# Adding the output bias by an adding transfer instead of by matmuls, in an adaLN block with a gated recurrence and experts

## The chip, the cores and the metric

One core of a Trainium2 chip runs the whole kernel. The metric is device time in microseconds (us) of one execution. Its engines have short names in the profile: PE is TensorE (PEld its weight loads), DVE is VectorE, ACT is ScalarE, POOL is GpSimd, SP is SyncE, which here only issues transfers.

## What is computed

The input x has 4 samples of 2048 tokens with 256 channels. The part that the change touches is the first half, the gated linear recurrence and its residual:

```python
h = _layernorm(x, axis=-1) * (1 + ca) + sa
x = x + ga * _L0_attn_ref(h, ...)          # ends with: return h @ W_out + b_out
h = _layernorm(x, axis=-1) * (1 + cb) + sb
x = x + gb * _L0_ffn_ref(h, ...)           # 8 experts, each takes 512 tokens of a sample
```

Inside the recurrence stand three products (input, gate a, gate x), a scan along the tokens, and the output product with its bias. `ga` is a vector for each sample (kept at least 0.25 from zero), so `ga * (h @ W_out + b_out)` is `h @ (W_out * ga) + ga * b_out`. The second half chooses tokens by a softmax over 8 experts, and runs two-layer experts on them.

## The kernel before

The kernel has two blocks, one after the other. The first (the recurrence stage, up to about 358 us) works on 16 groups of 512 tokens (NG = 16, 4 groups to a sample, GB = 4), each group as 4 tiles of 128 tokens (TT = 4). The second block is the expert layers and runs to the end.

The first block is a software pipeline. In step s (the loop variable `s`) the engines work on five groups at once: group a = s is loaded and normalised, c = s - 1 goes through the three products, r = s - 2 through the scan, d = s - 3 through the output product and the residual, e = s - 4 through the expert scores. Each engine has its own program, written out by hand; semaphores order them, and each engine takes its instructions strictly in turn.

TensorE, in step s: the transposes of the normalised rows of c (into psT), the transposes of x1 of e, `project(d)` (line 1205), the product with Wa (which waits for `lo_z` of c), the product with Wx, the scores of e, and the product with Wu. From step 9 on, the choice of the first sample's tokens goes along: a search bit by bit, for which VectorE compares (line 217), TensorE sums the hits by a tiny matmul (line 293), and VectorE decides (lines 224 to 229), four rounds in a step. The first count of a step is issued in the middle of the product with Wa.

VectorE, in step s: `gated_u(r)` (lines 863 and 870; it waits for ScalarE's root `sc_t` and for the product with Wu), `lo_z(c)` (852), `scan(r)` (883), `residual(d)` (894, it adds the output product in psO to the rows of x in `x_buf`, and takes statistics), `stats1(a)`, `clip(c)` (901), `norm1(a)` (842, it waits for GpSimd's `rstd1(a)`), in step 1 `setup_out` (line 1007 on), and `keep_scores(e)` (908). The rows of x stay as they were loaded, in one of five buffers `x_buf`, until the residual; `norm1` writes its result to `z1`. SP loads a buffer again when the residual of five groups before is done.

ScalarE, in step s: `hi_z(c)`, then `gate_a(c)` (tanh and two exps of the product with Wa), `gate_x(c)` and the root for the scale (791), with table loads between them. GpSimd has little to do: `rstd2(d)` (lines 684 to 690) on the statistics of the residual, then `rstd1(a)` (675 and 677). At the end, in step NG + 2, it issues the first gathers of expert rows (line 440), in `fetch`.

The bias `ga * b_out` reaches the output on TensorE: `setup_out` makes `bias_hi` and `bias_rows`, where rows 0 to 63 hold the rounded part and rows 64 to 127 the rest of the bias of each sample, and `pick`, a 128 x 128 matrix with ones in rows 0 and 64. In `project` a matmul of `pick` with `bias_rows` opens the accumulation of each tile (line 1213), before two products of h with Wout (line 1215; each is recorded as two). psO is one accumulator, so `project(d)` waits for residual(d - 1).

Of the kernel before, what the change touches and what calls it, by code (L numbers as in the profile page):

```python
# [6 lines left out]
F32 = mybir.dt.float32  # L7
F32R = mybir.dt.float32r
BF16 = mybir.dt.bfloat16
I32 = mybir.dt.int32  # L10
ALU = mybir.AluOpType
# [3 lines left out]
P = 128  # L15
# [33 lines left out]
def adaln_kernel(nc, x, W_in, b_in, W_gx, b_gx, W_ga, b_ga, a_param, W_out, b_out, gate_w, w1, w2, c, wmod, out):  # L49
    B, S, D = x.shape  # L50
# [30 lines left out]
    with keep:  # L81
# [3 lines left out]
        def sem(name):  # L85
            return keep.enter_context(nc.semaphore(name))
# [367 lines left out]
        def sbr(name, shape, dt=F32):  # L454
            return recur.enter_context(nc.sbuf_tensor(name, shape, dt))
# [28 lines left out]
        Wx = [sbr(f"Wx{q}", [P, KD, D], F32R) for q in range(2)]  # L484
        Wa = [sbr(f"Wa{q}", [P, KD, D], F32R) for q in range(2)]
        Wout = [sbr(f"Wout{n}", [P, KD, D]) for n in range(2)]
        bias_hi = sbr("bias_hi", [P, B, D], F32R)
        bias_rows = sbr("bias_rows", [P, B, D], F32R)
        pick = sbr("pick", [P, P], F32R)
        Gb = sbr("Gb", [P, B, KD, E])  # L490
        sb_bc = sbr("sb_bc", [P, B, E])
        ca1 = sbr("ca1", [P, B, KD])
# [85 lines left out]
        r_p = sem("scaled_u_ready")  # L578
        r_b = sem("b_ready")
        r_hs = sem("h_ready")  # L580
        r_O = sem("out_in_psum")
        r_x1 = sem("x1_ready")
        r_st2 = sem("stats2_read")
# [21 lines left out]
        with nc.Block() as block:  # L605
# [53 lines left out]
            def _(pool):  # L659
# [10 lines left out]
                def rstd1(g):  # L670
# [5 lines left out]
                    pool.wait_ge(r_rs1, 2 * g + 1)  # L676
                    pool.tensor_tensor(rs1[g % 2][:], ve1[:], mhalf[:], ALU.pow).then_inc(r_rs1, 1)

                def rstd2(g):

                    pool.wait_ge(r_mv2, g + 1)
                    if g >= 1:
                        pool.wait_ge(r_nm2, 2 * g)
                    pool.tensor_scalar(ve2[:], x1[g % 2][:, :, D + 1], EPS, None, ALU.add).then_inc(r_rs2, 1)  # L684
                    pool.wait_ge(r_rs2, 2 * g + 1)
                    pool.tensor_tensor(x1[g % 2][:, :, D + 1], ve2[:], mhalf[:], ALU.pow).then_inc(r_rs2, 1)
                    pool.wait_ge(r_rs2, 2 * g + 2)
                    pool.tensor_tensor(ve2[:], x1[g % 2][:, :, D], x1[g % 2][:, :, D + 1], ALU.mult).then_inc(r_nm2, 1)
                    pool.wait_ge(r_nm2, 2 * g + 1)
                    pool.tensor_scalar(x1[g % 2][:, :, D], ve2[:], -1.0, None, ALU.mult).then_inc(r_nm2, 1)  # L690

                pool.wait_ge(s_one, 5)
                for s in range(LAST + 1):
# [13 lines left out]
                        rstd2(d)  # L707
                    if a is not None:
                        rstd1(a)
                    if s == NG + 2:  # L710
                        fetch(pool, 0)
                fetch(pool, 1)
# [95 lines left out]
            def _(dve):  # L808
# [78 lines left out]
                def residual(g):  # L887

                    dve.wait_ge(r_O, g + 1)
                    if g >= 2:  # L890
                        dve.wait_ge(r_x1s[g % 2], 16 * (g // 2))
                        dve.wait_ge(r_T2, g - 1)
                        dve.wait_ge(r_sr, g - 1)
                    dve.tensor_tensor(x1[g % 2][:, :, 0:D], O_tok, x_buf[g % XR][:], ALU.add).then_inc(r_x1, 1)
                    dve.wait_ge(r_x1, g + 1)
                    stats(g, x1[g % 2], st2, x1[g % 2][:, :, D:D + 2], r_st2, r_mv2)
# [111 lines left out]
                def setup_out():  # L1008

                    signed(psO[:].rearrange("p h (q d) -> p (h q) d", d=D), ga_bc, s_ga, 1)  # L1010
                    dve.wait_ge(s_bo, 16)
                    dve.tensor_tensor(g_mag[:], ga_bc[:], bout_bc[:].unsqueeze(1).to_broadcast([P, B, D]), ALU.mult).then_inc(s_ga, 1)
                    dve.wait_ge(s_ga, 5)
                    dve.tensor_copy(bias_hi[:], g_mag[:]).then_inc(s_ga, 1)
                    dve.wait_ge(s_ga, 6)
                    dve.tensor_copy(bias_rows[0:64], bias_hi[0:64].bitcast(F32))
                    dve.tensor_tensor(bias_rows[64:128], g_mag[64:128], bias_hi[64:128].bitcast(F32), ALU.subtract).then_inc(s_ga, 1)
                    dve.wait_ge(s_ga, 7)
                    dve.memset(pick[:].bitcast(F32), 0.0).then_inc(s_ga, 1)
                    dve.wait_ge(s_ga, 8)  # L1020
                    dve.memset(pick[0:1].bitcast(F32), 1.0)
                    dve.memset(pick[64:65].bitcast(F32), 1.0).then_inc(s_ga, 1)
                    dve.wait_ge(s_w["out"], 16)
                    scale_w_out(0)

# [80 lines left out]
            def _(pe):  # L1106
# [96 lines left out]
                def project(d):  # L1203

                    pe.wait_ge(r_hs, d + 1)
                    pe.wait_ge(s_wo, d // GB + 1)
                    if d == 0:
                        pe.wait_ge(s_ga, 9)
                        pe.wait_ge(s_gbs, 4)
                    if d >= 1:  # L1210
                        pe.wait_ge(r_x1, d)
                    for t in range(TT):
                        pe.matmul(O_tok[:, t, :], pick[:], bias_rows[:, d // GB, :], start=True, stop=False)
                        for k in range(KD):
                            ins = pe.matmul(O_tok[:, t, :], hs[d % 2][:, k, t * P:(t + 1) * P], Wout[d // GB % 2][:, k, :],  # L1215
                                            start=False, stop=(k == KD - 1))
                    ins.then_inc(r_O, 1)

                def turn_x1(g):
# [623 lines left out]
```

## Time and profile before

| | |
|---|---|
| median of 3 runs | 1168.9 us (1168.67 to 1169.73) |
| the profiled execution | 1173.53 us, its span 1171.7 us |
| mean granted TensorE clock | 0.951 of full |
| PE busy | 1075.5 us, 92% of the span |
| ACT busy | 756.4 us, 65% |
| DVE busy | 741.6 us, 63% |
| POOL busy | 428.3 us, 37% |
| stage of the recurrence | up to about 358 us |

Busy time is that of the engine's own instructions. A busy engine is not always the one that sets the time: what counts is which wait ends last. In the rows further on, a timeline row gives start, duration, engine, line and operation, output and inputs, the count of instructions in it, and in brackets how long the engine was idle before the first of them, and what ended that.

### The profile page before, as it was taken

What the parts mean: (1) busy time and instruction counts of PE and PEld (TensorE: products, weight loads), DVE (VectorE), ACT (ScalarE), POOL (GpSimd) and SP (SyncE); (2) the same over time, 40 slices, a digit from 0 to 9 for tenths busy, and PEclk for the clock granted to TensorE, in tenths of its full rate; (3) what the DMA queues carried; (4) which work ended last, traced back from release to release, by engine and by line L of the source; (5) the groups of instructions that cost most, each with busy time, mean ns of one, the idle gap of its engine ahead of it and who ended that gap; (6) DMA issues with size and microseconds to landing.
All of it is one profiled execution on the core that took longest, in us unless ns stands there. A gap on an engine that the chain in (4) does not pass through costs nothing.

```text
span 1171.7 us, 18741 instructions
## 1 busy us (share of the span) xinstructions
PE 1075.5 (92%) x6986; PEld 949.9 (81%) x6986; DVE 741.6 (63%) x1711; ACT 756.4 (65%) x1194; POOL 428.3 (37%) x384
## 2 busy tenths in 40 slices
PE   6579999999974999999999999999999999999993
PEld 5467878777863889988899889998999899988883
DVE  3658887989865788877545445545453554446665
ACT  2337666557615788776776677667776776676661
POOL 1012221212131345454443545454445453543542
PEclk8779998999976999999999999999999999999997
DMA  6004534221016545455522433334234432378971
GB/s 220 0 1 132 178 125 113 80 62 55 30 55 71 144 115 150 118 118 143 120 52 43 106 59 88 78 69 96 51 79 82 82 85 45 60 194 252 276 276 79
DMA packets 88443, 122.45 MB, mean 105 GB/s; under 512 B 17057, under 2 KB 74017, under 8 KB 87329
## 3 DMA queue, kind: packets, MB, share of 16 engines
q1 hardware_dynamic: 61456, 83.96, 22.4%
q0 software_dynamic: 24576, 36.37, 17.3%
q8 instruction: 55, 0.90, 0.3%
q10 hardware_dynamic: 2320, 0.93, 0.3%
q14 instruction: 36, 0.29, 0.1%
HBM read 78.96 MB, written 42.27 MB: 103 GB/s over the span
## 4 chain that ended last, share of the span: by engine, by line
PE 58%; DVE 6%; ACT 2%; issue 2%; POOL 1%; DMA 0%; POOLq 0%; ACTq 0%; DVEq 0%
PE psum L1763 29%; PE psum L1788 26%; PE psum L1739 2%; DVE w_raw L1609 1%; DVE hidT L1655 1%; DVE scratch L1613 1%; PE psum L420 1%; DVE w L1603 1%; ACT rows_in L1559 1%; ACT hf L1582 1%; POOL out_x L1489 1%; DVE place L402 0%; ACT acc L1541 0%; DVE res_t L1613 0%; DMA out_x<-scratch 0%
## 5 line engine op out<-in xcount | busy, mean ns | idle before, releaser
L1763 PE MATMUL psum<-w,hidT 128*128 128x256 f32 x3072 | 374.7, 284 | 11.7 <-DVE hidT L1655 11.7
L1763 PEld LDWEIGHTS psum<-w,hidT 128*128 128x128 f32 x3072 | 367.1, 192 | 13.4 <-DVE hidT L1655 13.1
L1788 PE MATMUL psum<-xT,w 128*128 128x512 f32 x1536 | 372.1, 398 | 0.3 <-DVE xT L1642 0.3
L1655 DVE TENSOR_TENSOR hidT<-hf,hidT 128x512 fp32r<-128x512 f32 x256 | 175.5, 692 | 265.9 <-ACT hidT L1586 265.7
L1788 PEld LDWEIGHTS psum<-xT,w 128*128 128x128 f32 x1536 | 285.8, 190 | 59.5 <-DVE xT L1642 0.7
L1461 POOL DMA_INDIRECT ffn_rows<-rows_y,idx_cur x120 | 205.4, 1711 | 229.5 <-issue 167.5
L440 POOL DMA_INDIRECT rows_in<-x_rows,idx_cur x128 | 138.3, 1081 | 187.2 <-DVE idx_cur L413 157.1
L1530 ACT ACTIVATE rows_y<-psum,g_cur 128x256 f32<-128x256 f32 x128 | 53.7, 469 | 190.7 <-PE psum L1763 190.7
L1586 ACT ACTIVATE hidT<-hf 128x512 fp32r<-128x512 f32 x256 | 161.8, 632 | 8.1
L1582 ACT ACTIVATE hf<-psum 128x512 f32<-128x512 f32 x256 | 150.6, 588 | 22.7 <-PE psum L1788 13.6
L760 ACT ACTIVATE ta<-psum,half_ba 128x512 f32<-128x512 f32 x32 | 20.3, 684 | 103.7 <-PE psum L1111 103.7
L684 POOL TENSOR_SCALAR ve<-x 128x4 f32<-128x4 f32 x16 | 3.7, 229 | 223.2 <-DVE x L826 223.2
L402 DVE TENSOR_TENSOR place<-row_id,slot_u 128x1024 bf16<-128x1024 bf16 x64 | 76.1, 1222 | 1.1
L1559 ACT ACTIVATE rows_in<-rows_in 128x256 f32<-128x256 f32 x128 | 66.3, 594 | 14.8 <-PEq L605 14.8
L1603 DVE TENSOR_TENSOR w<-w_raw,w 128x1024 fp32r<-128x1024 f32 x60 | 71.2, 1221 | 3.3 <-ACT w L1552 3.2
L1642 DVE TENSOR_TENSOR xT<-xf,xT 128x1024 fp32r<-128x1024 f32 x32 | 39.2, 1226 | 45.7 <-ACT xT L1518 45.7
L1111 PE MATMUL psum<-hT_z,Wa 128*128 128x512 f32 x192 | 54.9, 437 | 13.6 <-DVE hT_z L852 13.6
L1215 PE MATMUL psum<-Wout,hs 128*128 128x256 f32 x256 | 66.5, 392 | 0.0
L1552 ACT ACTIVATE w<-w_raw 128x1024 fp32r<-128x1024 f32 x60 | 59.7, 1045 | 8.4 <-DMA w_raw<-in_L_ffn_w 8.4
L1111 PEld LDWEIGHTS psum<-hT_z,Wa 128*128 128x128 f32 x192 | 38.4, 205 | 22.2 <-DVE hT_z L852 14.2
L1111 PE MATMUL psum<-hT_z,Wu 128*128 128x512 f32 x192 | 51.7, 414 | 0.0
L1215 PEld LDWEIGHTS psum<-Wout,hs 128*128 128x128 f32 x256 | 46.1, 198 | 5.2
(201 smaller groups left out, 1252.1 us busy)
## 6 DMA issues: line engine op xcount, KB each, us to landing
w_raw<-in_L_ffn_w SPq DMA_DIRECT2D x30, 1024.0 KB, 6.0
x_rows<-x SPq DMA_DIRECT2D x16, 516.0 KB, 3.8
x_buf<-in_L_attn_x SPq DMA_DIRECT2D x16, 512.0 KB, 5.9
ffn_rows<-scratch SPq DMA_DIRECT2D x8, 1024.0 KB, 8.3
w_raw<-ffn_rows SPq DMA_DIRECT2D x16, 512.0 KB, 8.9
scratch<-x_rows SPq DMA_DIRECT2D x12, 512.0 KB, 6.8
out_x<-scratch SPq DMA_DIRECT2D x12, 512.0 KB, 4.4
rows_in<-x_rows,idx_cur POOLq DMA_INDIRECT x136, 2.9
```

What stands on the lines that cost most here:

```text
L402: dve.tensor_tensor(place[n][:, at, :], row_id[:].unsqueeze(1).to_broadcast([P, ST // 2, P]), slot_u[n][:, at, :].to_broadcast([P, ST // 2 ...
L440: pool.indirect_dma_start(rows_in[u % 2][:, t, :], None, xr_dram[b], bass.IndirectOffsetOnAxis(ap=idx_cur[u % 4][:, t:t + 1], axis=0))\
L1111: ins = pe.matmul(out_, stationary(qs, k), moving(qm, k), start=(first and j == 0), stop=(last and j == len(terms) - 1))
L1215: ins = pe.matmul(O_tok[:, t, :], hs[d % 2][:, k, t * P:(t + 1) * P], Wout[d // GB % 2][:, k, :], start=False, stop=(k == KD - 1))
L1461: pool.indirect_dma_start(acc_dram[b], bass.IndirectOffsetOnAxis(ap=idx_cur[u % 4][:, t:t + 1], axis=0), rows_y[u % 2][:, t, :], None, com ...
L1559: ins = act.activation(x_u[:, t, 0:D], x_u[:, t, 0:D], ACT.Identity, bias=x_u[:, t, D:D + 1], scale=x_u[:, t, D + 1:D + 2])
L1582: act.activation(hf[m % HF][:], H_bank[m % 4], ACT.Gelu_apprx_tanh).then_inc(f_hf, 1)
L1586: act.activation(hidT[0][:, m, :], hf[m % HF][:], ACT.Copy).then_inc(f_hh, 1)
L1603: dve.tensor_tensor(parts[1][:, at, :], raw[:, at, :], parts[0][:, at, :].bitcast(F32), ALU.subtract).then_inc(f_ws, 1)
L1655: dve.tensor_tensor(hidT[1][:, m, :], hf[m % HF][:], hidT[0][:, m, :].bitcast(F32), ALU.subtract).then_inc(f_hl, 1)
L1763: ins = pe.matmul(y_tile(u, t), hidT[qs][:, k, t * P:(t + 1) * P], w2_s[n % 2][qm][:, k, :], start=(x_ == 0), stop=(x_ == len(terms) - 1))
L1788: ins = pe.matmul(H_bank[m % 4], w1_s[n % 2][qs][:, k, m * P:(m + 1) * P], xT[qm][:, k, :], start=(x_ == 0), stop=(x_ == len(terms) - 1))
```

## The change

The matmul with `pick` leaves `project`; the first product with Wout now opens the accumulation. The tensors `bias_hi`, `bias_rows` and `pick` are gone, with the VectorE instructions that made them and with TensorE's wait for them. In their place `setup_out` writes `ga * b_out` in full precision, the same on all 128 partitions, to `bias_bc`. In each step s from 1 to 16 GpSimd, after `rstd1(s)`, issues a transfer that adds `bias_bc` of the sample to all four tiles of group s - 1 in `x_buf` (128 partitions x 4 tiles x 1 KB, 512 KB in all). It waits for `norm1` of this group, for `bias_bc` once, and for the transfer of two groups before. `residual(g)` has a new wait for it.

```diff
-        bias_hi = sbr("bias_hi", [P, B, D], F32R)
-        bias_rows = sbr("bias_rows", [P, B, D], F32R)
-        pick = sbr("pick", [P, P], F32R)
+        bias_bc = sbr("bias_bc", [P, B, D])
@@
+                def add_bias(g):
+
+                    pool.wait_ge(r_z1, g + 1)
+                    if g == 0:
+                        pool.wait_ge(s_ga, 5)
+                    if g >= 2:
+                        pool.wait_ge(r_xb[g % 2], 16 * (g // 2))
+                    pool.dma_start(x_buf[g % XR][:], bias_bc[:, g // GB:g // GB + 1, :].to_broadcast([P, TT, D]),
+                                   accum_op=ALU.add).then_inc(r_xb[g % 2], 16)
@@
+                    if 1 <= s <= NG:
+                        add_bias(s - 1)
@@
+                    dve.wait_ge(r_xb[g % 2], 16 * (g // 2 + 1))
                     dve.tensor_tensor(x1[g % 2][:, :, 0:D], O_tok, x_buf[g % XR][:], ALU.add).then_inc(r_x1, 1)
@@
-                    dve.tensor_tensor(g_mag[:], ga_bc[:], bout_bc[:].unsqueeze(1).to_broadcast([P, B, D]), ALU.mult).then_inc(s_ga, 1)
-                    dve.wait_ge(s_ga, 5)
-                    dve.tensor_copy(bias_hi[:], g_mag[:]).then_inc(s_ga, 1)
-                    dve.wait_ge(s_ga, 6)
-                    dve.tensor_copy(bias_rows[0:64], bias_hi[0:64].bitcast(F32))
-                    dve.tensor_tensor(bias_rows[64:128], g_mag[64:128], bias_hi[64:128].bitcast(F32), ALU.subtract).then_inc(s_ga, 1)
-                    dve.wait_ge(s_ga, 7)
-                    dve.memset(pick[:].bitcast(F32), 0.0).then_inc(s_ga, 1)
-                    dve.wait_ge(s_ga, 8)
-                    dve.memset(pick[0:1].bitcast(F32), 1.0)
-                    dve.memset(pick[64:65].bitcast(F32), 1.0).then_inc(s_ga, 1)
+                    dve.tensor_tensor(bias_bc[:], ga_bc[:], bout_bc[:].unsqueeze(1).to_broadcast([P, B, D]), ALU.mult).then_inc(s_ga, 1)
@@
                     if d == 0:
-                        pe.wait_ge(s_ga, 9)
                         pe.wait_ge(s_gbs, 4)
@@
-                        pe.matmul(O_tok[:, t, :], pick[:], bias_rows[:, d // GB, :], start=True, stop=False)
                         for k in range(KD):
                             ins = pe.matmul(O_tok[:, t, :], hs[d % 2][:, k, t * P:(t + 1) * P], Wout[d // GB % 2][:, k, :],
-                                            start=False, stop=(k == KD - 1))
+                                            start=(k == 0), stop=(k == KD - 1))
```

## Rows read from the trace of the kernel before

**Rows 1.** Page, head and section 2: span; tenths for 40 slices

```profile
span 1171.7 us, 18741 instructions
...
PE   6579999999974999999999999999999999999993
...
PEclk8779998999976999999999999999999999999997
```

**Rows 2.** Waits, 60 to 320 us: us in total, times, longest

```profile
DVE z L842 <- POOL rs L677: 10.4, 12, 1.6
...
DVE flip L226 <- PE psum L293: 5.2, 8, 0.8
...
DVE p_t L863 <- ACT sc_t L791: 4.3, 4, 2.0
```

**Rows 3.** Timeline, weight loads of `project(4)` in step 7

```profile
148.00 0.19 PEld L1213 LDWEIGHTS psum<-bias_rows,pick 128*128 128x128 f32 x1
...
148.88 0.19 PEld L1213 LDWEIGHTS psum<-bias_rows,pick 128*128 128x128 f32 x1
...
149.10 0.74 PEld L1215 LDWEIGHTS psum<-Wout,hs 128*128 128x128 f32 x4
...
151.83 2.71 PEld L1111 LDWEIGHTS psum<-hT_z,Wa 128*128 128x128 f32 x12
```

**Rows 4.** Timeline, `setup_out` in step 1 and the start behind it

```profile
47.43 1.22 DVE L1012 TENSOR_TENSOR scratch<-ga_bc,bout_bc 128x1024 f32<-128x1024 f32 x1
...
52.10 0.69 DVE L936 TENSOR_TENSOR Wout<-out_raw,ga_bc 128x512 f32<-128x512 f32 x1
...
56.74 4.85 PE L1111 MATMUL psum<-hT_z,Wa 128*128 128x512 f32 x12 [13.39 <-DVE hT_z L852]
```

**Rows 5.** Timeline, VectorE, steps 4, 6 and 8

```profile
98.54 1.41 DVE L863 SCALAR_TENSOR_TENSOR p_t<-psum,bias_u,sc_t 128x512 f32<-128x512 f32 x2 [2.01 <-ACT sc_t L791]
...
130.97 1.41 DVE L863 SCALAR_TENSOR_TENSOR p_t<-psum,bias_u,sc_t 128x512 f32<-128x512 f32 x2 [1.68 <-ACT sc_t L791]
...
175.20 0.29 DVE L203 TENSOR_REDUCE total<-scratch 128x16 f32<-128x128 f32 x1 [0.62 <-ACT scratch L317]
```

**Rows 6.** Timeline, step 10: `lo_z` and the start of the product with Wa

```profile
204.02 1.40 DVE L852 SCALAR_TENSOR_TENSOR hT_z<-psum,ca,hT_z 128x512 fp32r<-128x512 f32 x2
...
206.95 1.74 PE L1111 MATMUL psum<-hT_z,Wa 128*128 128x512 f32 x6
```

**Rows 7.** Timeline, step 16 and the tail of the stage

```profile
323.37 0.16 DVE L265 COPY first_slot<-psum 128x1 f32<-128x1 f32 x1 [1.26 <-PE psum L304]
...
332.08 0.55 PE L1213 MATMUL psum<-bias_rows,pick 128*128 128x256 f32 x1 [2.18 <-DVE x L894]
...
340.02 0.17 DVE L409 COPY lists<-psum 128x8 f32<-128x8 f32 x1 [3.31 <-PE psum L420]
...
340.70 1.22 DVE L894 TENSOR_TENSOR x<-psum,x_buf 128x1024 f32<-128x1024 f32 x1
...
346.98 1.22 POOL L440 DMA_INDIRECT rows_in<-x_rows,idx_cur  x1 [0.19 <-issue]
```

**Rows 8.** GpSimd: timeline of rstd2; line 1461, durations in ns, landings

```profile
123.84 0.23 POOL L684 TENSOR_SCALAR ve<-x 128x4 f32<-128x4 f32 x1 [12.08 <-DVE x L826]
...
319.82 0.55 POOL L690 TENSOR_SCALAR x<-ve 128x4 f32<-128x4 f32 x1
...
L1461 POOL DMA_INDIRECT ffn_rows<-rows_y,idx_cur x120: 1552/1574/2576, 398.7 to 1105.6; - x120
...
DMA to landing us min/median/max: 3.7/4.1/7.2
```

**Rows 9.** Timeline, GpSimd's rstd1 beside VectorE's clip, step 15

```profile
302.97 0.66 DVE L901 TENSOR_SCALAR a_t<-a_t 128x1024 f32<-128x1024 f32 x1
...
303.14 0.58 POOL L675 TENSOR_SCALAR ve<-mv 128x4 f32<-128x4 f32 x1 [0.45 <-DVE mv L826]
```

**Rows 10.** Timeline, TensorE around the turned probabilities, step 8

```profile
176.15 0.33 PE L287 MATMUL psum<-ident,scratch 128*128 128x128 f32 x1 [2.71 <-DVE scratch L205]
...
179.22 5.03 PE L1111 MATMUL psum<-hT_z,Wu 128*128 128x512 f32 x12
```

More of the change, by code:

```diff
@@ L580, in adaln_kernel @@
         r_hs = sem("h_ready")
+        r_xb = [sem(f"x_with_bias{n}") for n in range(2)]
         r_O = sem("out_in_psum")
```

## The prediction

> **What bounds the kernel now.** I read the page first [rows 1]: the line of TensorE's busy tenths stands at 9 in nearly all of the 40 slices (29.3 us each), and the chain that ended last, further down the page, runs mostly through it. But the lines of that chain are those of the expert layers, which the change does not touch. The recurrence stage, up to there, needs its own reading. So I took the table of waits for 60 to 320 us [rows 2]. VectorE (DVE) waits there for very little: eight times for the hit counts from TensorE (5.2 us in total), four times for ScalarE's square root (4.3 us), twelve times for GpSimd's reciprocal root (10.4 us). All else it computes without a break. So VectorE's order of work sets the length of a step of this loop, and TensorE counts only where VectorE waits for something that hangs on it. That gives the rule for the sum: a saving of X on TensorE per step gives back, per step, the smaller of X and VectorE's wait for TensorE's chain. The GpSimd waits are no part of that: the chain there is residual, statistics, rstd2, rstd1, norm1, all timed by VectorE's own residual, and shorter TensorE work leaves it alone.
>
> **Part 1, the matmuls with `pick`.** 4 tiles times 16 groups go. In the timeline of one `project` [rows 3] the weight loads, not the matmuls, are the pace: 20 loads lie between 148.00 and 151.83, 3.83 / 20 = 0.19 us each, and the load behind `pick` starts 149.10 - 148.88 = 0.22 us after it. Four of them: 0.77 by the mean, 0.88 by the single distance. I take 0.8 us for each group, since the first of each four hides partly behind the transposes.
>
> **Part 2, the setup.** After the product `ga_bc * bout_bc` (47.43 + 1.22 = 48.65) VectorE made hi and lo parts and the selector until `scale_w_out` began at 52.10 [rows 4]. That is 3.45 us, and the next thing that everybody waits for is behind it: TensorE had sat idle 13.39 us when VectorE's `lo_z` released it at 56.74. Nothing else is late in that stretch, so 3.4 us come off whole. TensorE's restart at the low clock afterwards stays, since its idle is still 10 us.
>
> **Part 3, steps 3 to 8.** ScalarE's chain (tanh, two exps, tanh, root) starts when the product with `Wa` ends, and this product starts when `project` has ended. So the root comes 0.8 us earlier for each step. VectorE's waits for it are 2.01 us in step 4 and 1.68 us in step 6 [rows 5]; the other two of the four share what is left of 4.33, 0.64 us [rows 2]. By the rule: 0.8 + 0.8 + 0.64 = 2.24 us. In step 8 VectorE waits 0.62 us for the exp of the scores, which is behind the same chain on ScalarE; there TensorE has run ahead by about 0.55 us more than VectorE, so 0.55 goes. Sum 2.8 us. The product could not start earlier than `lo_z` allows: in steps 3, 5, 7 and 8 that is done well before `project` ends, and in step 4, where TensorE waits for it already, it comes forward by the same 0.8 us as VectorE's step.
>
> **Part 4, steps 9 to 16.** Here VectorE waits each step for the first count, which TensorE issues in the middle of the product with `Wa`. In step 10 `lo_z` ended at 204.02 + 1.40 = 205.42, while the product began only at 206.95 [rows 6]: `project` holds it, with 1.5 us to spare, so 0.8 us come through. The eight waits sum to 5.2 us and none is over 0.8 [rows 2], so all of them go: 5.2 us. In step 16 TensorE's last sum of the choice keeps VectorE for 1.26 us [rows 7]; its 0.8 less the 0.65 already counted there gives 0.15. Sum 5.3 us.
>
> **Part 5, the tail.** `project(15)` begins when residual(14) frees the accumulator (332.08), runs mostly at the low clock, and VectorE waits 3.31 us for the list matmul behind it [rows 7]. Then residual(15), rstd2(15) and GpSimd's first gather at 346.98 follow, and the gathers end the stage. So four picks come off the path: 0.8 us if the clock returns at the same moment, 1.5 us if all four fall in the slow stretch. I take 0.8.
>
> Sum: 3.4 + 2.8 + 5.3 + 0.8 = 12.3 us. Not all of 16 * 0.8 + 3.4 = 16.2 us arrive, since in most steps VectorE has less to wait for than TensorE saves.
>
> **Part 6, the adding transfer.** The trace shows no direct adding transfer from GpSimd. The nearest row is the indirect adding one of the experts, for 128 rows of 1 KB [rows 8]: GpSimd is busy 1.55 to 2.58 us with it, median 1.57. The new one names 512 such rows. Lower bound 1.55 us (cost per instruction), upper bound 4 * 2.58 = 10.3 us (cost per row, all slow); below nothing is excluded, as an instruction is added. I take 4 * 1.57 = 6.3 us, as it is near in kind and four times in rows. It stands after rstd1 in each step. Behind it on GpSimd is rstd2 of the next step, which now comes after 12.08 us of idle time [rows 8] and would after the change come after some 11.3 us. So even the upper bound is covered; cost on the path 0. If that cover went, every us over it would be paid in some 13 steps.
>
> Landing: 3.7 to 7.2 us for 128 rows [rows 8]; times four gives 29 us as an end that I think far too long, the same as one gives 3.7. I take some 10 us. The one that waits is `residual`, two steps later. The tightest is group 15: issued behind rstd2(13) at 319.82 + 0.55 = 320.4, wanted by residual(15) at 340.70 [rows 7, 8], 20 us. With issue and landing at 6.3 + 10 it holds with 4 us to spare, and the groups before it have over 25 us. `add_bias(0)` waits for the bias rows, which VectorE has by 48.65; behind it on GpSimd is only rstd1(2), wanted 12 us later. In step s the wait for `r_z1` is for the step before, long met, and so is the wait for the transfer of two groups ago. SP's queue is not touched; the x loads reuse a buffer only after its residual, as now.
>
> Two rules of the Trainium skill bear on this part. A GpSimd instruction beside VectorE's clip (302.97 to 303.63) took 0.58 us [rows 9], one like it alone 0.23 [rows 8]. The Trainium skill, "SBUF — State Buffer", section "Who interferes with whom", says that VectorE in its two-port modes locks GpSimd out, descriptor writing too; the trace agrees for this compute instruction. By that rule the issue would stretch by the fast copies beside it, a share of a us in a step; the sum stays, the chance of the slow rival grows a little. Its page "DMA: Bandwidth & Descriptors", section "Anatomy of one DMA", gives about 2.0 us plus bytes over 436 GB/s for a transfer from GpSimd: an estimate of 3.2 us for 512 KB, against my 10.
>
> **Rivals.** (A) Forecast: all as above, 1168.9 - 12.3 = 1156.6 us. (B) A further stretch at the low clock: in step 8 TensorE sat idle for 2.71 us, and the 12 matmuls with `Wu` after it took 5.03 us [rows 10], where six of that kind took 1.74 in step 10 [rows 6]; PEclk falls by a tenth there [rows 1]. That is 1.5 us lost, and with the scores that ran in the same stretch I take 3. The change gives TensorE longer idle stretches (0.15 us more in steps 9 to 16, 0.8 more before `project(15)`). For: the longer pause. Against: the pauses in the loop stay under 1.7 us, and those of 1.5 us are followed by full clock now. One more such stretch in the loop costs 3: 1159.6; two, 1162.6. (C) The loop gives back nothing, since some work of VectorE or of GpSimd that I take as fixed stretches beside the new transfer and its issue (8 MB more in SBUF, GpSimd busy beside the scan). Only the setup's 3.4 us are left: 1165.5. Against: the clip in [rows 9] kept its 0.66 us while GpSimd worked beside it; it was GpSimd that waited. (D) The other side: the issue is longer than GpSimd's idle time of 11.3 us. Then rstd2 and rstd1 come late, and norm1 behind them, on VectorE's path. Each us over 11.3 costs 13 us; from 12.3 us of issue on the kernel is slower than before. At 13 us of issue it is 1.7 * 13 = 22 us against 12.3: 1178.7. For: 512 rows are four times what has been seen. Against: even four of the longest are 10.3. (E) The transfer is late only for group 15 (landing over 14 us): some 5 us lost, 1161.6, still faster.
>
> **How the numbers follow.** The profiled execution has a span of 1171.7 [rows 1] and a time of 1173.5 us; the median of the runs is 1168.9. A saving in absolute us carries over, so the median becomes 1156.6 and a profile's span 1159.4. Chances: A 0.66, B 0.12, E 0.05, C 0.08, D 0.06, other 0.03. A's own range is 1154.5 to 1158.5: 0.88 instead of 0.77 for each group and 1.5 in the tail below, a few tenths lost at each step above. The range over B and E is 1153.5 to 1163, which leaves C, D and the rest out. Within 0.2% (2.3 us, about what a measurement of this kernel can tell from no change) is 0.04, slower 0.07, faster 0.89.
>
> **What would show it.** In the profile after: the product with `Wa` of step 2 starts about 3.4 us earlier (53.3); the weight loads of `project` span some 3.05 us; VectorE's waits for the counts of TensorE are gone, those for GpSimd's root are unchanged at 10 us; the last gather of the stage ends 12 us earlier; residual shows no wait for a DMA. Wrong: a residual released by a DMA (E), a norm1 that waits longer for GpSimd (D), longer matmuls with a fall in PEclk before 300 us (B), or VectorE operations longer than in [rows 5, 6] (C).

## The result, and the profile after

The median went from 1169.32 us (1168.67 to 1174.28, 6 runs) to 1163.61 us (1162.29 to 1165.46, 6 runs): a ratio of 0.9947, 95% interval 0.9928 to 0.9965. The change makes the kernel faster, by 5.7 us and not by the 12.3 us forecast, and the time lies 0.6 us above the upper end of the range.

The page of the kernel after, head, section 2 and the queue that carries GpSimd's transfers in section 3, answers to [rows 1]:

```profile
span 1161.8 us, 18640 instructions
...
PEclk8789999999967999999999999999999999999997
...
q0 software_dynamic: 33024, 44.75, 22.1%
```

The granted clock keeps its shape; the seventh digit, an 8 in [rows 1], is a 9 (176 to 205 us, step 8 and what follows it). The span is 9.9 us shorter than in [rows 1], 4.2 us more than the medians say. The profiled execution of the kernel before (1173.5 us) was one of its longer ones: its executions fall on two levels, near 1169 and near 1174 us. Queue q0 carries 8.4 MB more than before (36.37 MB), the bytes of the new transfers.

The waits of VectorE from 60 to 320 us (waited for: us in total, times, longest), beside [rows 2]:

```profile
DVE z L853 <- POOL rs L676: 12.2, 13, 1.6
...
DVE p_t L874 <- ACT sc_t L802: 1.5, 2, 1.0
DVE flip L226 <- PE psum L293: 1.5, 7, 0.3
```

The waits for the counts fell from 5.2 to 1.5 us, not to nothing; those for ScalarE's root from 4.3 to 1.5. Those for GpSimd's root, forecast to stay at 10 us, grew from 10.4 to 12.2. Lines are shifted: 853 is `norm1`, 863 `lo_z`, 874 the first of `gated_u`, 906 `residual`, 1215 `project`, 685 the new transfer.

The weight loads of `project(4)`, timeline, beside [rows 3]:

```profile
144.67 3.32 PEld L1215 LDWEIGHTS psum<-Wout,hs 128*128 128x128 f32 x16
148.02 2.71 PEld L1113 LDWEIGHTS psum<-hT_z,Wa 128*128 128x128 f32 x12
```

Now 3.35 us to the next load instead of 3.83: 0.48 us less. The setup, timeline of VectorE, beside [rows 4]:

```profile
48.03 1.22 DVE L1024 TENSOR_TENSOR bias_bc<-ga_bc,bout_bc 128x1024 f32<-128x1024 f32 x1
49.17 0.68 DVE L948 TENSOR_TENSOR Wout<-out_raw,ga_bc 128x512 f32<-128x512 f32 x1
...
52.35 1.41 DVE L863 SCALAR_TENSOR_TENSOR hT_z<-psum,ca,hT_z 128x512 fp32r<-128x512 f32 x2
```

The transfer itself: the group of line 685 on GpSimd (durations in ns, least, median, most) and its landing, and VectorE's `norm1` from 60 to 320 us:

```profile
L685 POOL DMA_DIRECT2D x_buf<-bias_bc x16: 1339/1350/1567, 49.9 to 313.1; - x16
...
DMA to landing us min/median/max: 5.2/6.6/12.9
```

```profile
L853 DVE TENSOR_SCALAR z<-x_buf,mv,rs x56: 394/415/591, 62.8 to 298.9; 128x256 f32<-128x256 f32 x56
```

The issue is short (1.35 us against 6.3 taken), the landing too, and no residual waits for it. But single `norm1` instructions take up to 591 ns. The same group in the kernel before reads:

```profile
L842 DVE TENSOR_SCALAR z<-x_buf,mv,rs x56: 405/409/416, 65.1 to 305.9; 128x256 f32<-128x256 f32 x56
```

The timeline of step 12 shows what lies beside it (kernel after):

```profile
244.22 1.06 POOL L676 TENSOR_TENSOR rs<-ve,mhalf 128x4 f32<-128x4 f32 x1
...
245.25 1.35 POOL L685 DMA_DIRECT2D x_buf<-bias_bc  x1
245.32 1.71 DVE L853 TENSOR_SCALAR z<-x_buf,mv,rs 128x256 f32<-128x256 f32 x4 [0.55 <-POOL rs L676]
```

The order `rstd1(s)`, then the transfer, means that the end of one GpSimd instruction releases `norm1` on VectorE and the issue on GpSimd together. The four `norm1` take 1.71 us; in the same step before they took

```profile
252.12 1.38 DVE L842 TENSOR_SCALAR z<-x_buf,mv,rs 128x256 f32<-128x256 f32 x4 [0.55 <-POOL rs L677]
```

That is 0.33 us in a step, and `norm1` is on the path of VectorE. It happens in 13 steps, 3 to 15. In step 2 the issue ended at 60.51 us and `norm1` began only at 62.75. There the issue pushed GpSimd's later index instructions and its memset back to beside `clip`, which took 1.25 us instead of 0.69; VectorE's next wait for TensorE became 0.55 us shorter, so this cost nothing.

### The profile page after: what moved, and what is told of

Its sections match the earlier page's. It is cut to its first block, busy times and chain, and to the rows that moved or that the text cites. A ratio compares the mean times of both kernels' runs of the same rounds, so it can differ in the third digit from the quotient of the medians.

```text
span 1161.8 us, 18640 instructions
## 1 busy us (share of the span) xinstructions
PE 1062.8 (91%) x6922; PEld 937.9 (81%) x6922; DVE 742.7 (64%) x1705; ACT 756.5 (65%) x1194; POOL 452.5 (39%) x400
## 4 chain that ended last, share of the span: by engine, by line
PE 58%; DVE 6%; ACT 2%; issue 2%; POOL 1%; DMA 0%; POOLq 0%; ACTq 0%; DVEq 0%
PE psum L1763 29%; PE psum L1788 26%; PE psum L1739 2%; DVE w_raw L1609 1%; DVE hidT L1655 1%; DVE scratch L1613 1%; PE psum L420 1%; DVE w L1603 1%; ACT rows_in L1559 1%; ACT hf L1582 1%; POOL out_x L1489 1%; DVE place L402 0%; ACT acc L1541 0%; DVE res_t L1613 0%; DMA out_x<-scratch 0%
## 5 line engine op out<-in xcount | busy, mean ns | idle before, releaser
L1215 PE MATMUL psum<-Wout,hs 128*128 128x256 f32 x256 | 60.2, 390 | 2.7 <-DVE x L906 2.7
L1215 PEld LDWEIGHTS psum<-Wout,hs 128*128 128x128 f32 x256 | 49.1, 197 | 9.1 <-issue 2.7
```

## The experiments

Three theories. T1: the issue of the transfer, beside `norm1`, holds VectorE; that is what is missing. T2: the bytes do it (8 MB more read, added and written in SBUF, into the rows that VectorE reads). T3: nothing is lost to the transfer; the gain was overestimated, in the matmuls or by the choice of executions.

**Both kernels again.**

> The kernel before, once more, for a second profile. Open: the first profile of it took 1173.5 us where the median is 1169.3, while that of the changed kernel took its own median. If the first profile was a late one in the recurrence stage, the last gather of the stage now ends some 4 us earlier than 357.9 us. If it was late in the expert layers, it ends at 357.9 again and the rest is shorter. If profiling itself costs 4.5 us in this kernel, the span is 1171.7 again.

> The changed kernel once more, beside the two below on one chip. Before took 1168.5 to 1169.5 us or 1173.7 to 1174.7 us in its runs, so the comparison hangs on which of the two a run falls into. If the changed kernel has such a second level too, some of its runs lie 4 to 5 us from 1163.6; if not, all lie within 1162.3 to 1165.5. A VectorE step from lo_z to lo_z at full clock: 17.23 us again (before: 17.39).

Before: 1167.41 us, one run; its last gather ended at 355.34 us, 1.6 us earlier and not 4, and the rest was 4.5 us shorter. After: 1163.69 us (1160.93 to 1166.68, 8 runs), ratio 0.996 (0.9944 to 0.9976); its runs spread over 5.7 us without two clear levels. The steps from 9 on are reproduced to hundredths of a us; the two profiles of before differ by 6 us all the same. TensorE from 350 to 410 us (length, busy, granted clock, share of the DMA engines, GB/s), first before, then before again:

```profile
350.00:410.00 60.00, 41.89 (x243) 0.77 0.57 109
```

```profile
350.00:410.00 60.00, 41.49 (x250) 0.82 0.55 104
```

The same program gets a different share of the clock there, and in the tail of the stage too. So each profile is compared by stretches: the first of the four instructions of VectorE that make `ga_bc` (42.52 us in the kernel before), `lo_z` of steps 2, 8, 9 and 16, the copy of the list (340.02 in [rows 7]), the end of the last gather of the stage, the end of the span. The columns are the distances between these points, in us:

| kernel | setup to 2 | 2 to 8 | 8 to 9 | 9 to 16 | to list | to gather | to the end |
|---|---|---|---|---|---|---|---|
| before | 12.76 | 110.26 | 21.39 | 122.62 | 30.47 | 16.93 | 814.8 |
| before_again | 12.77 | 110.30 | 21.37 | 122.64 | 27.99 | 16.93 | 810.3 |
| after | 9.23 | 109.42 | 19.26 | 121.57 | 28.45 | 16.88 | 813.9 |
| after_again | 9.23 | 109.22 | 19.26 | 121.58 | 30.09 | 16.88 | 815.3 |
| no_transfer | 9.23 | 108.57 | 19.29 | 119.27 | 29.85 | 16.93 | 811.8 |
| no_transfer2 | 9.23 | 108.02 | 19.27 | 119.28 | 29.76 | 16.95 | 811.7 |
| picks_out | 12.77 | 108.06 | 19.28 | 119.28 | 29.65 | 16.96 | 812.1 |
| picks_out2 | 12.76 | 108.95 | 19.28 | 119.28 | 29.80 | 16.95 | 812.0 |
| transfer_alone | 13.00 | 112.37 | 21.37 | 124.94 | 30.97 | 16.85 | 815.3 |
| behind_norm | 9.24 | 108.58 | 19.29 | 119.29 | 29.85 | 16.87 | 811.5 |
| behind_norm2 | 9.23 | 108.77 | 21.83 | 119.57 | 28.51 | 16.90 | 813.7 |
| beside_scan | 9.22 | 108.42 | 19.27 | 119.31 | 29.76 | 16.91 | 815.2 |
| two_tiles | 9.24 | 109.21 | 19.27 | 120.96 | 28.74 | 16.89 | 814.5 |
| one_tile | 9.23 | 108.87 | 21.81 | 119.56 | 28.52 | 16.88 | 813.9 |

The columns "setup to 2" and "9 to 16" repeat to 0.02 us between two profiles of one program, but for behind_norm2 (0.28 us over behind_norm in "9 to 16", with the longer "8 to 9" ahead of it; one_tile has both too). "2 to 8" varies by up to 0.9 us, "to list" and "to the end" by up to 2.5 and 4.5 us. The loop decides between the theories.

**The change without its transfer.**

```diff
-                    if 1 <= s <= NG:
-                        add_bias(s - 1)
@@
-                    dve.wait_ge(r_xb[g % 2], 16 * (g // 2 + 1))
```

> The changed kernel without the adding transfer and without the wait for it: the output lacks the bias. Theory 1 (the issue on GpSimd holds up VectorE's norm1, which starts at the same moment) and theory 2 (the moved bytes hold it up): norm1 is back at 1.38 us for its four instructions, 0.33 less in each of 14 steps, and the time is 4 to 4.5 us under the changed kernel's, about 1159.3. Theory 3 (the longer norm1 is covered, and the gain is small for another reason): about 1163.6, as with the transfer.

1159.29 us (1158.38 to 1159.95, 4 runs), ratio 0.989 (0.986 to 0.992). Its groups of `norm1` and its wait for the counts, 60 to 320 us:

```profile
L851 DVE TENSOR_SCALAR z<-x_buf,mv,rs 128x256 f32<-128x256 f32 x56 | 19.4, 410 | 12.2 <-POOL rs L676 12.2
```

```profile
DVE flip L226 <- PE psum L293: 1.4, 7, 0.3
```

`norm1` is back at its old duration; "9 to 16" falls by another 2.30 us, seven times 0.33. So the transfer costs 4.3 us of the median (1163.6 less 1159.3, measured on two chips), and T3 is not all of it. The gain without any transfer is 10.0 us against the 1169.3 of the kernel before, not 12.3. The medians alone don't settle that: beside this run the kernel before had a median of 1173.69 us, more of its executions being long ones, and the interval of the ratio reaches past 12.3 us. The loop does: the waits for the counts stay at 1.4 us, so a part of the sum was too large as well.

**The transfer alone**, of the same size in the same place, added to the kernel before, with another source and another destination:

```diff
+                def add_apart(g):
+                    pool.wait_ge(r_z1, g + 1)
+                    if g == 0:
+                        pool.wait_ge(s_ga, 4)
+                    if g >= 1:
+                        pool.wait_ge(r_xd, 16 * g)
+                    pool.dma_start(apart_x[:], ga_bc[:, g // GB:g // GB + 1, :].to_broadcast([P, TT, D]),
+                                   accum_op=ALU.add).then_inc(r_xd, 16)
@@
                         rstd1(a)
+                    if 1 <= s <= NG:
+                        add_apart(s - 1)
```

> The kernel before, bias on TensorE as it was, with one more adding transfer of the same size in the same place, from ga_bc to a buffer apart that nobody reads; nobody but the next such transfer waits for it. Theories 1 and 2: norm1 takes 1.71 us in place of 1.38, the time is 4 us over before, about 1173.5. Here the wait for the counts (0.65 us a step) stays. Theory 2 in its narrow form (writes to x_buf disturb reads of x_buf): no change, as the bytes go elsewhere. Theory 3: no change, 1169.3.

1177.03 us (1175.79 to 1178.36, 10 runs), ratio 1.0039 (1.0023 to 1.0056): 3.3 us over the 1173.69 of the kernel before beside it, where 4 were forecast. Its step 12 and its `norm1` as a group:

```profile
254.61 1.35 POOL L690 DMA_DIRECT2D apart_x<-ga_bc  x1
254.68 1.71 DVE L860 TENSOR_SCALAR z<-x_buf,mv,rs 128x256 f32<-128x256 f32 x4 [0.55 <-POOL rs L681]
```

```profile
L860 DVE TENSOR_SCALAR z<-x_buf,mv,rs 128x256 f32<-128x256 f32 x56 | 23.5, 481 | 9.5 <-POOL rs L681 9.4
```

The same 1.71 us, though no byte goes to the rows of x, and "9 to 16" is 2.32 us longer than before. It is not a meeting on `x_buf`. Whether issue or bytes hold VectorE, the trace of the kernel after tells too. In step 12 `norm1` ran from 245.32 to 247.02 us. Queue q0, which carries this transfer, moved no packet from 245.25 to 247.55 us, where only the queue of SP's transfers had any; then all its 528 came (packets, MB, share of the 16 engines, first from 245.25 to 247.55, then from 247.55 to 252.00 us):

```profile
q1 hardware_dynamic: 522, 0.52, 94.1%
```

```profile
q0 software_dynamic: 528, 0.52, 73.9%
```

In step 3 the first packet came even at 98.37 us, 4 us after `norm1` (92.44 us, 1.72 us long) had ended. So `norm1` was held before a byte of the transfer moved.

**The same transfer, issued behind `norm1`**: with all its bytes, behind the norm of its own group. Run twice.

```diff
-                    if 1 <= s <= NG:
-                        add_bias(s - 1)
+                    if s == 1:
+                        add_bias(0)
+                    if 1 <= s < NG:
+                        add_bias(s)
```

> The changed kernel, with the transfer for group s issued in step s, behind its norm1 (for group 0 still in step 1, ahead of that for group 1): GpSimd waits until norm1(s) has ended, so the issue lies beside keep_scores and gated_u, and not beside norm1. Theory 1: norm1 back at 1.38 us, 4 to 4.5 us under the changed kernel, about 1159.3. Theory 2 (bytes): about the same as the changed kernel, 1163.6, since the same bytes are in flight beside VectorE. A rival to both: the issue holds up whatever VectorE starts beside it, and the 0.33 us move to gated_u: 1163.6 with another instruction longer.

> The issue behind norm1, once more, for a comparison with the changed kernel on one chip. Theory 1 (the issue held up norm1 by 0.33 us in 14 steps): 4.3 us under after_again by the trace; the runs have two levels, 1158 to 1159 and 1162 to 1164, so by the medians between 0 and 5 us. The step stays at 16.90 us.

1162.46 us (1158.16 to 1164.04, 6 runs), ratio 0.9916 (0.9889 to 0.9942), and 1162.47 us (1159.7 to 1163.6), ratio 0.9945 (0.993 to 0.9961). Step 12 in the first:

```profile
243.08 1.38 DVE L855 TENSOR_SCALAR z<-x_buf,mv,rs 128x256 f32<-128x256 f32 x4 [0.55 <-POOL rs L676]
...
244.77 1.35 POOL L685 DMA_DIRECT2D x_buf<-bias_bc  x1 [1.72 <-DVE z L855]
...
245.16 1.41 DVE L876 SCALAR_TENSOR_TENSOR p_t<-psum,bias_u,sc_t 128x512 f32<-128x512 f32 x2
```

The issue takes the same 1.35 us, `norm1` its 1.38, the `gated_u` that now lies beside the issue its 1.41, and "9 to 16" is that of the kernel without any transfer. With that and the late packets T2 falls, and T1 stands: it is where the issue lies. The stage is as short as without the transfer, but the median is 3.2 us above that of no_transfer, and on the chip where both ran it is only 1.2 us below that of after_again (1162.47 and 1163.69 us, the ranges overlap). In the first of the two profiles, of one of the shortest runs (1159.08 us), nothing of this is to be seen (811.5 us "to the end"), in the second "8 to 9" and the end are longer. What those 3 us are is open. So the hold-up is shown for the loop. That the median gets all of it back was not.

**How much of the issue holds VectorE.** The transfer cut to one tile of four, and to two:

```diff
-                    pool.dma_start(x_buf[g % XR][:], bias_bc[:, g // GB:g // GB + 1, :].to_broadcast([P, TT, D]),
+                    pool.dma_start(x_buf[g % XR][:, 0:1, :], bias_bc[:, g // GB:g // GB + 1, :],
```

```diff
-                    pool.dma_start(x_buf[g % XR][:], bias_bc[:, g // GB:g // GB + 1, :].to_broadcast([P, TT, D]),
+                    pool.dma_start(x_buf[g % XR][:, 0:2, :], bias_bc[:, g // GB:g // GB + 1, :].to_broadcast([P, 2, D]),
```

> The changed kernel, with the transfer for one tile of the four only (128 rows of 1 KB, not 512); three tiles lack the bias. Theory 1a: norm1 is held up by the issuing instruction as such: norm1 1.71 us again, step 17.23 us, GpSimd's issue about 1.3 us. Theory 1b: it is held up by the writing of the descriptors, in proportion to the rows: the issue is shorter and norm1 takes 1.46 us, step 16.98. Theory 2 (moved bytes): as 1b for norm1, but with the issue as long as before.

> The changed kernel with the adding transfer cut to two of the four tiles of a group (256 rows named; two tiles are left without the output bias). With four tiles the issue takes 1.35 us and norm1 1.71 us; with one tile 0.94 us and 1.38 us. If the hold-up grows with the rows behind a fixed first part of the issue, the issue takes about 0.94 + 0.41 / 3 = 1.08 us and norm1 1.38 + 0.33 / 3 = 1.49 us. If the hold-up appears at once with what lies behind some 0.94 us, norm1 takes 1.71 again. If only the last rows do it, it stays at 1.38.

1163.40 and 1163.70 us, one run each. The groups of the issue and of `norm1`, first of one tile, then of two:

```profile
L685 POOL DMA_DIRECT2D x_buf<-bias_bc x16: 927/940/1146, 49.6 to 312.6; - x16
```

```profile
L853 DVE TENSOR_SCALAR z<-x_buf,mv,rs x56: 396/408/416, 62.1 to 298.6; 128x256 f32<-128x256 f32 x56
```

```profile
L685 POOL DMA_DIRECT2D x_buf<-bias_bc x16: 1248/1258/1472, 49.9 to 312.1; - x16
```

```profile
L853 DVE TENSOR_SCALAR z<-x_buf,mv,rs x56: 394/414/544, 62.6 to 298.1; 128x256 f32<-128x256 f32 x56
```

The two times say nothing of the hold-up: one_tile, without any, took as long as the kernel after, with the longer "8 to 9" (21.81 us). With one tile nothing is held: neither a hold-up that comes with every issue nor one in proportion to the rows fits. With two tiles the four `norm1` of a late step take 1.61 or 1.62 us, with four 1.71. So against 0.94, 1.26 and 1.35 us of issue stand 0, 0.24 and 0.33 us of hold-up: none of the three forecasts for two tiles (1.49, 1.71 or 1.38 us), but the same difference in both longer cases, 1.26 - 0.24 = 1.02 and 1.35 - 0.33 = 1.02. In amount that is what the issue takes beyond some 1.0 us. It is not that part of the time in which VectorE stands still: in the kernel after, the loss falls on the two middle ones of the four, and the first of these had ended by 246.20 us, 0.95 us after the issue began, with 0.15 us of the loss in it. By the window from 245.90 to 246.20 us:

```profile
L853 DVE TENSOR_SCALAR z<-x_buf,mv,rs x2: 554/570/585, 245.6 to 246.1; 128x256 f32<-128x256 f32 x2
```

The last starts at 246.63, when the issue has ended (246.60), and takes 395 ns. Why the amount follows the issue's length so is open.

**The issue beside `lo_z` and the scan**, the third place:

```diff
                     pool.wait_ge(r_z1, g + 1)
+                    pool.wait_ge(r_b, g + 1)
```

> The changed kernel, complete, with one more wait: the transfer of group s - 1 is issued only when VectorE's gated_u of that group is done, so that the issue lies beside lo_z and the scan instead of norm1. All theories: norm1 back to 1.38 us for its four instructions. If only instructions like norm1 (their input from SBUF alone, with factors per partition) are held, lo_z stays at 1.40 us and the scan at 2.34 us for two, the step takes 16.9 us as with the issue beside keep_scores. If any VectorE work beside the issue's later part is held, lo_z or the scan takes 0.3 us more and the step stays at 17.2 us.

1161.76 us, one run. Its step 12, timeline:

```profile
229.91 1.40 DVE L864 SCALAR_TENSOR_TENSOR hT_z<-psum,ca,hT_z 128x512 fp32r<-128x512 f32 x2
230.54 1.36 POOL L686 DMA_DIRECT2D x_buf<-bias_bc  x1 [5.33 <-issue]
231.23 0.34 DVE L217 TENSOR_SCALAR_CACHE_REDUCE hit<-scratch,cand 128x128 bf16<-128x128 f32 x1
231.49 0.09 DVE L217 DVE_READ_ACCUMULATOR hit<-scratch,cand 128x1 bf16 x1
231.49 2.46 DVE L895 TENSOR_TENSOR_SCAN hs<-a_t,hs,b_t 128x512 f32<-128x512 f32 x2
```

Nothing beside the issue is longer than elsewhere. In the kernel after, the held instructions lay from 0.40 to 1.46 us behind the start of the issue. Here that stretch (230.94 to 232.00) holds the second `lo_z`, the compare `hit` (0.34 us, 0.35 in the kernel after) and the start of the scan, whose 2.46 us it takes in the same step of the kernel behind_norm too, where no issue lies there. "9 to 16" is 119.31. So of what lay in this stretch, `norm1`, `p_t`, `lo_z`, `hit` and the scan, only `norm1` was held. The compare and the scan work in SBUF alone as well, so that is not what sets `norm1` apart. The Trainium skill, "SBUF — State Buffer", "Who interferes with whom", offers a cause: `tensor_scalar` can enter the modes of VectorE in which it takes the pair of ports that it shares with GpSimd, and then whichever of the two holds the pair first blocks the other; an instruction with one SBUF input outside these modes does not contend. `p_t` (1.41 us with and without) agrees with it; the scan has two SBUF inputs, so this sentence does not cover it. Three rows don't fit so simply. The block is to last for the whole instruction, but an issue of 0.94 us that also began 0.07 us ahead of `norm1` held nothing, and one of 1.35 us held only 0.33 us. And `norm1` does not show the pace of such a mode: its instructions of 256 elements per partition follow each other after 0.32 us, while `clip`, a `tensor_scalar` too, does 1024 in 0.66 us. So that the ports are the cause is not shown.

**The matmuls alone, and the setup**: the kernel before without its matmuls with `pick`, its setup kept, and the kernel without the transfer beside it on one chip.

```diff
-                        pe.matmul(O_tok[:, t, :], pick[:], bias_rows[:, d // GB, :], start=True, stop=False)
@@
-                                            start=False, stop=(k == KD - 1))
+                                            start=(k == 0), stop=(k == KD - 1))
```

> The kernel before without the 64 matmuls with pick, all else kept, the seven instructions on VectorE too; the output lacks the bias. It parts the gain of no_transfer (10 to 14 us under before) into matmuls and setup. As I had it: setup 3.4 us, so this is 3.4 us over no_transfer, 1162.7, with lo_z of step 2 at 55.3 to 56 as in before. By the traces so far project saves 0.56 us and not 0.8 (3.27 us instead of 3.83), so the step at full clock is 16.90 us, as in no_transfer. Rival: the setup's 3.4 us are found again later in a wait; then the time is that of no_transfer, 1159.3.

> The changed kernel without the adding transfer and without the wait for it (the output lacks the bias), again, now timed beside the next one on one chip. Same as in its first run: 1159.3 us within 2 us, the four norm1 at 1.38 us, a step of 16.9 us.

> The kernel before without its matmuls with pick but with the instructions of the setup (the output lacks the bias), beside the last one on one chip; the two differ in the setup alone. If the 3.4 us of the setup come off the median whole, this one is 3.4 us above the kernel without the transfer: 1162.7. If a later stage gives part of them back (the gathers ended 2.1 us apart in the two profiles), it is 2 us above it: 1161.3. The one profile of each cannot tell a part given back from another place of the stretches at the low clock; three rounds on one chip can.

picks_out: 1164.04 us (1161.83 to 1167.93, 10 runs), ratio 0.9964 (0.9945 to 0.9982); again 1163.98 us (1162.12 to 1165.06, 6 runs), ratio 0.9947 (0.9928 to 0.9966). no_transfer2: 1158.35 us (1158.12 to 1158.92, 4 runs), ratio 0.9897 (0.987 to 0.9925), where the kernel before had 1169.2. On this one chip the medians part the gain of 10.85 us: 1169.2 - 1164.0 = 5.2 us for the matmuls, 1164.0 - 1158.35 = 5.6 us for the setup. The setup's own stretch is 3.53 us shorter in every pair (12.76 to 9.23). The other 2.1 us are neither of the two values expected: in the profiles 0.8 us are an earlier start of the execution, before anything differs (the instruction that begins `ga_bc` starts at 42.98 and 42.14 us), and 0.9 us lie in "2 to 8". Neither belongs to the setup: in the other pair of profiles (picks_out and no_transfer) the kernel with the setup starts 0.7 us earlier and its "2 to 8" is 0.5 us shorter. A cause for the 2.1 us was not tried. And 1163.6 - 1158.35 = 5.3 us, with the first run 4.3, are the price of the transfer, between medians of different chips.

## Why the prediction was right in direction and wrong in size

The account by medians: removals 10.0 to 10.9 us against 12.3 forecast, the transfer 4.3 to 5.3 us against 0. Together 5.7.

**Part 6, the step that failed.** It asked how long GpSimd is busy and who waits for GpSimd, found cover (11.3 us of idle time, 1.35 used) and wrote a cost of 0 on the path. It did not ask who works beside the issue. The issue stands directly behind the instruction that releases `norm1`, so the two meet in every step from 3 to 15, and the reading of [rows 2] had said that everything VectorE does in this loop is on the path. The price is 13 meetings (steps 3 to 15): 23.5 - 19.4 = 4.1 us of busy time, some 0.33 us in each. From `lo_z` of step 2 to that of step 16 the kernel after takes 2.9 to 3.7 us more than the one without the transfer; part of the 4.1 is absorbed, as in step 8, where VectorE waits for TensorE behind `norm1` (19.26 and 19.29 us in "8 to 9"). Of the 4.3 to 5.3 us by medians that is the part that is shown. Rival C named just this mechanism, VectorE's fixed work stretched beside the issue, and got 0.08. What was held against it was one row where GpSimd was the one that waited [rows 9], a compute instruction and not an issue. The rule that was weighed beside it was read in one direction only, VectorE locking GpSimd out; the same section of the Trainium skill says that who comes first keeps the ports. The runs show that other direction, VectorE held by an issue that started 0.07 us before it (245.25 and 245.32), though not that ports are the reason. The row bounds of the same part were far off harmlessly: 1.35 us of issue for 512 rows lies below the lower bound of 1.55, so that rows named are not what an issue costs, and the landing of 6.6 us lies between the 10 taken and the estimate of 3.2 from the Trainium skill, "DMA: Bandwidth & Descriptors", "Anatomy of one DMA". D and E fell with that.

**Part 1, the term that was mis-sized.** 0.8 us for four loads was their share of a mean distance. Measured: 0.48 us, since 16 loads now take 3.35 / 16 = 0.21 us each where 20 took 0.19. A load with `pick` cost 0.12 us at the margin, not 0.19: a mean over a mixed row of instructions is not what the removal of one kind gives.

**Part 4 follows its own rule with the right X.** The smaller of X and the wait is then about 0.5 us a step, not 0.65: the loop step without a transfer in the way shrank by 3.35 / 7 = 0.48 us (122.62 to 119.28), and 1.5 of 5.2 us of waits are left. With the hold-up 0.15 us a step are left of it, 1.05 us in seven steps where 4.6 (seven of the eight waits) were forecast. The rule was right, the size of X was not.

**Part 3** gave more than its 2.8 us, by luck in step 8: from `lo_z` of step 2 to that of step 9 the loop is 131.65 us before and 127.3 to 128.2 without the picks, 3.4 to 4.4 less. Steps 2 to 7 gave 1.3 to 2.3 us of it where 2.24 were forecast. Against the forecast that the waits for GpSimd's root are left alone, those of steps 4 and 6 grew from 0.93 to 1.56 us (picks_out as well as after), while two waits of 0.5 us of `clip` for ScalarE went. [rows 2] showed three of VectorE's waits, and the text beside it ("All else it computes without a break") was wrong: there are some 20 us more in the same window. Two of them stand in step 8, for TensorE: 1.7 us ahead of the scores (line 908) and 4.5 us ahead of `gated_u`. There the other 2.1 us lie, against 0.55 forecast: in the kernel after the first of these waits is gone and the second is 3.7 us. TensorE's pause before the turned probabilities kept its 2.71 us, but the 16 matmuls of the scores behind it took 1.86 us instead of 3.05 (granted clock 0.97 from 172 to 174 us, 0.59 from 176 to 180 before), and those with `Wu` are shorter than the 5.03 us of [rows 10]. Timeline of the kernel before, then after:

```profile
176.32 3.05 PE L1237 MATMUL psum<-Gb,x1T 128*128 128x8 f32 x16
...
184.34 1.41 DVE L863 SCALAR_TENSOR_TENSOR p_t<-psum,bias_u,sc_t 128x512 f32<-128x512 f32 x2 [4.47 <-PE psum L1111]
```

```profile
171.88 0.33 PE L287 MATMUL psum<-ident,scratch 128*128 128x128 f32 x1 [2.71 <-DVE scratch L205]
172.04 1.86 PE L1237 MATMUL psum<-Gb,x1T 128*128 128x8 f32 x16
173.76 4.59 PE L1113 MATMUL psum<-hT_z,Wu 128*128 128x512 f32 x12
...
178.44 1.41 DVE L874 SCALAR_TENSOR_TENSOR p_t<-psum,bias_u,sc_t 128x512 f32<-128x512 f32 x2 [3.73 <-PE psum L1113]
```

Rival B had asked only whether the clock would cost more. Two profiles (one_tile, behind_norm2) have 21.8 us in the column "8 to 9", as long as before, so this gain does not come each time. With the hold-up the whole of Part 3 is 3.0 to 3.2 us.

**Part 2** is right: 12.76 to 9.23 us, 3.53 against 3.4.

**Part 5** can't be told from the clock's share. The rows of the tail, kernel after, beside [rows 7]:

```profile
324.67 5.08 PE L1215 MATMUL psum<-Wout,hs 128*128 128x256 f32 x16 [2.66 <-DVE x L906]
...
331.05 0.17 DVE L409 COPY lists<-psum 128x8 f32<-128x8 f32 x1 [1.75 <-PE psum L420]
```

The same 16 matmuls took more without the transfer (granted clock 0.66 from 324 to 328 us, where the kernel after had 0.92 from 327 to 330):

```profile
321.05 6.51 PE L1212 MATMUL psum<-Wout,hs 128*128 128x256 f32 x16 [2.65 <-DVE x L903]
```

So the stretch "to list" is 27.99 to 30.47 us before and 28.45 to 30.09 us after, and no 0.8 us can be read from it. The 9.0 us by which the last gather ended earlier than in the first profile of before (356.95 to 347.93) hold 2.0 us from this stretch.

**From profile to median.** "A saving in absolute us carries over" is right only for profiles of the same level. The profile before was at 1173.5 us, 4.6 above its own median, and I had taken this as a constant offset. It was a longer tail and end: 30.47 and 814.8 us against 27.99 and 810.3 in its second profile, less 0.8 us by which the second started later.

**What would show it.** The line on operations longer than in [rows 5, 6] pointed the right way, though `norm1` was not among the rows listed there.

## What to carry to other kernels

Work moved to an idle engine is not free because it is short and covered: ask what the critical engine does during it, above all where both are released by the same event, and move the issue to a place where it does not meet such work. Here, behind the norm, the loop step fell from 17.2 to 16.9 us at full clock, though the median on one chip fell by only 1.2 us. Price a removed instruction by the distances around its own kind, not by the mean of a mixed row. And before setting the profile's time against the median, look whether that execution was a long or a short one.

## What the runs showed of the hardware

- GpSimd's issue of a direct adding transfer in SBUF took 0.94 us for 128 rows of 1 KB, 1.26 for 256 and 1.35 for 512, the landing 4.1, 4.6 and 6.6 us (medians).
- An issue beside four `tensor_scalar` of 128x256 f32 in SBUF held VectorE: by 0, 0.24 and 0.33 us, in both longer cases as much as the issue took beyond 1.02 us. It did so before a packet of its transfer moved. The issue itself was not longer for it (1.35 us with and without). Instructions with an input from PSUM (1.41 us), the compare (0.34 us) and the scan (2.46 us with and without) were not held.
- Sixteen f32 weight loads of 128x128 beside matmuls of 128x256 take 3.35 us, twenty with the same matrix loaded every fifth time 3.83.
- One program's profiles differ by 6 us: 2.5 us in the tail of the stage and 4.5 us behind it, less 0.8 us at the start, with the granted clock at 0.77 or 0.82 from 350 to 410 us.
